# Two fused transformer layers: the work between layer zero and layer one dealt in another order

## What is computed

```
# layer 0: adaptive RMS norm, 8 query heads of 64, one key/value head, then a gated MLP of 2048
h   = x * rsqrt(mean(x*x) + 1e-6) * (ln1_w * (1 + cond @ ln1_tw.T))
q, k, v = h @ Wq.T, h @ Wk.T, h @ Wv.T        # q and k turned by their positions (rope)
x   = x + softmax(q k' / 8) v @ Wo.T
h2  = x * rsqrt(mean(x*x) + 1e-6) * (ln2_w * (1 + cond @ ln2_tw.T))
x   = x + (silu(h2 @ Wg.T) * (h2 @ Wu.T)) @ Wd.T
# layer 1: adaptive layer norm, 16 query heads of 32, 4 key/value heads through a latent of 128
y   = (x - mean(x)) * rsqrt(var(x) + 1e-5) * (1 + scale(cond)) + shift(cond)
q   = y @ Wq.T;  c = y @ Wkd.T;  k, v = c @ Wku.T, c @ Wvu.T
x   = x + softmax(q k' / sqrt(32)) v @ Wo.T
```

## Time and profile before

| what | value |
|---|---|
| median of 3 runs | 871.74 us (870.44, 871.74, 877.64) |
| the profiled execution | 878.93 us |
| span of its instructions | 877.1 us |
| TensorE busy in the span | 850.0 us (97%) |
| mean granted TensorE clock | 0.988 |

### The profile page before, as it was taken

One profiled execution on the slowest core, in us unless ns is written; L12 is line 12 of the kernel. 1 busy time (PEld: TensorE's weight loads), 2 busy tenths in 40 slices (PEclk: granted clock), 3 DMA queues, 4 the chain that ended last, 5 costly groups with the idle time before them and its releaser, 6 DMA issues.

```text
span 877.1 us, 15477 instructions
## 1 busy us (share of the span) xinstructions
PE 850.0 (97%) x5864; PEld 707.8 (81%) x5864; DVE 596.7 (68%) x877; ACT 443.1 (51%) x819; POOL 404.3 (46%) x320
## 2 busy tenths in 40 slices
PE   9798999999999999999999899999999999999997
PEld 6686888888888888888787788888878878887885
DVE  6686466766765766666457777876757857768874
ACT  4665445455445455444447456465463454445652
POOL 2456546455454455547357446354344434422330
PEclk9899999999999999999999999999999999999998
DMA  9901534534523524524534346446245264240001
GB/s 341 347 30 41 160 104 141 159 102 138 169 101 103 175 94 117 175 95 122 192 121 120 119 136 186 146 137 187 93 157 161 97 181 136 76 119 13 26 26 37
DMA packets 114297, 113.53 MB, mean 129 GB/s; under 512 B 57520, under 2 KB 80048, under 8 KB 114224
## 3 DMA queue, kind: packets, MB, share of 16 engines
q1 hardware_dynamic: 113504, 112.45, 40.2%
q10 hardware_dynamic: 720, 0.09, 0.1%
HBM read 88.15 MB, written 24.38 MB: 128 GB/s over the span
## 4 chain that ended last, share of the span: by engine, by line
PE 74%; DVE 8%; issue 6%; DMA 4%; ACT 3%; POOL 3%; SPq 1%; POOLq 0%; ACTq 0%; DVEq 0%
PE ps L684 23%; PE ps L686 22%; PE ps L685 22%; DMA turned_q<-tq 2%; PE ps L798 2%; PE ps L964 1%; DVE ex L1410 1%; DMA rwd<-WdT 1%; PE ps L730 1%; PE ps L721 1%; PE ps L775 1%; PE ps L941 1%; POOL qkr L592 1%; POOL qkr L591 1%; DMA pT<-turned_p 1%
## 5 line engine op out<-in xcount | busy, mean ns | idle before, releaser
L684 PE MATMUL ps<-h2h,guh 128*128 128x512 f32 x512 | 205.5, 401 | 3.1 <-issue 2.2
L686 PE MATMUL ps<-h2l,guh 128*128 128x512 f32 x512 | 201.1, 393 | 0.0
L685 PE MATMUL ps<-h2h,gul 128*128 128x512 f32 x512 | 201.0, 393 | 0.0
L544 POOL TENSOR_TENSOR gul<-rgu,guh 128x1024 fp32r<-128x1024 f32 x64 | 160.5, 2508 | 68.4 <-ACT guh L1746 68.4
L549 POOL TENSOR_TENSOR wdl<-rwd,wdh 128x512 fp32r<-128x512 f32 x64 | 82.9, 1296 | 145.3 <-ACT wdh L1754 145.3
L1309 DVE TENSOR_TENSOR xres<-ps,xres 128x512 f32<-128x512 f32 x128 | 87.6, 685 | 65.9 <-PE ps L686 65.4
L684 PEld LDWEIGHTS ps<-h2h,guh 128*128 128x128 f32 x512 | 96.9, 189 | 24.8 <-issue 3.9
L686 PEld LDWEIGHTS ps<-h2l,guh 128*128 128x128 f32 x512 | 96.9, 189 | 21.2
L685 PEld LDWEIGHTS ps<-h2h,gul 128*128 128x128 f32 x512 | 96.9, 189 | 19.7
L684 PE MATMUL ps<-wdh,ah 128*128 128x512 f32 x256 | 100.3, 392 | 2.8 <-DVE al L1304 1.7
L685 PE MATMUL ps<-wdh,al 128*128 128x512 f32 x256 | 99.7, 389 | 0.0
(11 more groups left out here) (178 smaller groups left out, 1676.9 us busy)
## 6 DMA issues: line engine op xcount, KB each, us to landing
rgu<-gu SPq DMA_DIRECT2D x64, 512.0 KB, 4.8
rwd<-WdT SPq DMA_DIRECT2D x64, 256.0 KB, 4.1
turned_q<-tq SPq DMA_DIRECT2D x20, 320.0 KB, 2.7
qkT<-turned_q SPq DMA_DIRECT2D x20, 320.0 KB, 3.7
turned_p<-tp SPq DMA_DIRECT2D x9, 512.0 KB, 2.6
pT<-turned_p SPq DMA_DIRECT2D x9, 512.0 KB, 3.9
xt<-xT SPq DMA_DIRECT2D x16, 256.0 KB, 3.5
out<-xres SPq DMA_DIRECT2D x15, 256.0 KB, 3.6
```

The source lines that it names most:

```text
L544: pool.tensor_tensor(gul[i][:, :], rgu[i][:, :], guh[i][:, :], ALU.subtract).then_inc(m_gul, 1)
L684: pe.matmul(dst, lh, rh, start=start, stop=False)
L685: pe.matmul(dst, ll, rh, start=False, stop=False)
L686: return pe.matmul(dst, lh, rl, start=False, stop=stop)
```

## The change

It touches the steps s = 15 to u = 0, SP's order in steps 0 to 8 and DVE's in step 9. No instruction is added or taken away on any engine, and the pieces keep their order; only what stands between them moves.

- `FILL1`: step -1 has (4, 2, 2, 2, 2) in place of (4, 4, 0, 4, 0), step 0 has (4, 2, 4, 2, 0) in place of (4, 2, 2, 2, 2). Both still have 12. Step 9 had five zeros and now falls to the default of five zeros.
- s = 15: ACT's `norm1(0)` stands behind the first fill, DVE's `turn_y(0)` behind the second, SP's `y_away(0)` behind the second, directly ahead of `y_back(0)`.
- u = 0 to 8: SP does `probs_back1(u)` ahead of `y_away(u+2)`. In u = -1 nothing changes by this.
- u = 9: DVE does its first two pieces (`add_down` parts 0 and 1 of the last pair) ahead of `rope_mul1(10)` and not behind it.

```diff
-FILL1 = {-1: (4, 4, 0, 4, 0), **{u: (4, 2, 2, 2, 2) for u in range(0, 9)}, 9: (0, 0, 0, 0, 0)}
+FILL1 = {-1: (4, 2, 2, 2, 2), 0: (4, 2, 4, 2, 0), **{u: (4, 2, 2, 2, 2) for u in range(1, 9)}}
 
@@ SP, steps s
                     queries_back(s + 1)
+                fill(pieces, f2)
                 if s == NT - 1:
                     y_away(0)
-                fill(pieces, f2)
-                if s == NT - 1:
                     y_back(0)
@@ SP, steps u
                 if 0 <= u < TAIL:
                     probs_away1(u)
+                    probs_back1(u)
                 if u < TAIL:
                     y_away(u + 2)
-                if 0 <= u < TAIL:
-                    probs_back1(u)
-                if u < TAIL:
                     y_back(u + 2)
@@ DVE, steps u
                     turn_probs1(u)
+                if u == TAIL:
+                    fill(pieces, 2)
                 if in_layer(u + 1):
                     rope_mul1(u + 1)
                 if u == TAIL:
-                    fill(pieces, 2)
                     probs_T1(u)
@@ ACT, steps s
-                if s == NT - 1:
-                    norm1(0)
                 fill(pieces, f1)
                 if s > HEAD and in_layer(s + 1):
                     values(s + 1)
+                if s == NT - 1:
+                    norm1(0)
```

## The result

The changed kernel takes 880.12 us (median of 13 runs, 875.45 to 882.11), the kernel before 872.79 us (median of 13, 868.95 to 879.70). The ratio is 1.0071 with a 95% interval of 1.0048 to 1.0093: slower by 4 to 8 us, where 3.2 us faster had been forecast. The profiled execution took 876.11 us (span 874.3), less than the 878.93 us of before. It is the spread of the runs that makes this so: the trace of before is one of its slowest executions, the trace of after one of the faster ones. A second trace of each was therefore taken; with them there are four to read.

A forecast was written before the change was run, and what follows sets the result against it. TensorE, busy in 97% of the span, was taken as the bound, leaving waits and low-clock stretches to remove. Terms -1.8 - 0.3 - 1.1 = -3.2 us, on the median 871.74, gave 868.5 us; range 863.5 to 874.5.

The forecast's parts named there:

- seam: From s = 15 to the gate behind the scores of step 1: 1.8 us faster, of 6.8 us removable.
- rounds: Steps u = 1 to 8: 0.3 us faster, from the second wait for probabilities; bounds -1.0 and +5.6 us.
- step 9: DVE's additions ahead of the rope: the 1.1 us wait of down 31,2 goes, 1.1 us faster.
- s = 15 and u = -1: Silu wait (0.9 us), queries' wait (1.7) and low clock of gate 37 (1.7) go; L1395 starts near 475.5.
- DVE in u = 0 and the scores of step 1: Scale 2.3 us earlier, still taking 3.42; scores of step 1 wait 3.8 us, to 505.5 in place of 508.21.
- second rival: In step 0 DVE's scale runs apart from POOL's subtraction, chain 2.2 us shorter: -5.4, 866.3 us; chance 0.10.
- third rival: Each round SP waits 2.6 us longer for y's store: rounds +5.6, net +2.4, 874.1 us; chance 0.16.
- The fourth: Seam keeps its time: scores of step 1 wait 5.5 us or clock falls twice; -0.3 to -1.4, 870.8; chance 0.17.
- The first: Both new waits fail to appear and all gains arrive: -10.6 us at most, some -9, 863 us; chance 0.09.

The follow-up runs named there:

- the three kernels with the queries first in the new fills: Whole change, queries' store ahead of y's fetch: 866.96 us; also y's store before probabilities' fetch: 867.48; or queries' store also before fill's weight load: 866.30.
- the norm alone: Kernel before with only the norm of tile 0 moved in s = 15 (ACT, DVE, SP): 870.58 us, ratio 0.9974.
- step 9 alone: Kernel before with only DVE's two pieces ahead of the rope in step 9: 872.42 us, ratio 0.9978.
- the kernel before with the queries first: Kernel before with SP's queries' store ahead of the fetch of y in steps -1 to 8: 877.16 us, ratio 1.0024.
- the two variants: Whole change, queries' store ahead of y's fetch, plus y's store before probabilities' fetch (867.48 us) or queries' store before the fill's weight load (866.30 us).

## Why the prediction was wrong

The sum was -1.8 (seam), -0.3 (rounds), -1.1 (step 9), and the gate behind the scores of step 1, with or without the low clock, was counted to the seam. In these terms the first trace of after has, against the first and the second of before: seam -4.5 and -0.7 up to the scores of step 1, with +1.7 behind them for the low clock; rounds +5.7 and +6.7 without that stretch; step 9 -1.3. One by one:

*Step 9: right.* -1.0 to -1.3 in the traces, -1.4 alone, by the mechanism named.

*s = 15 and u = -1: right in what it removed.* The silu wait, the queries' wait and the low clock of gate 37 all went. L1392 of step 0 was held back by `high_act(36)` behind the weight's cast, as said: `high_act(36)` starts 4.0 us behind the end of `high_y(1)` (I had counted 4.1), and L1392 2.6 us behind that (2.3). But the whole chain came 3.0 us sooner than I had put it (472.47 for 475.5); 1.7 of these the trace had ahead of s = 15, the rest I can't account for. One reading was incomplete: I called 2.5 and 1.7 us the two longest single waits of PE, and the full list also has two of 2.2 us, early in layer zero, which no edit touches.

*DVE in u = 0 and the scores of step 1: the mechanism right, the size not.* The chain was shorter than I counted (timeline of DVE, then of POOL, against the earlier trace rows):

```profile
481.66 1.22 DVE L1407 TENSOR_TENSOR ex<-ex,smx 128x1024 f32<-128x1024 f32 x1
482.91 2.02 DVE L1428 STREAM_TRANSPOSE tp<-ex 128x1024 f32<-128x1024 f32 x1
...
488.26 1.32 DVE L1421 STREAM_TRANSPOSE tq<-qkr 128x640 f32<-128x640 f32 x1 [0.26 <-POOL qkr L589]
```
```profile
482.05 3.10 POOL L541 TENSOR_TENSOR gul<-rgu,guh 128x1024 fp32r<-128x1024 f32 x1 [2.30 <-ACT guh L1743]
```

The scale took 1.22 us, the case of my second rival, though the reason that I gave there is not what happened: the two did start together, with the scale 0.4 us ahead. The queries' wait was 2.6 us and not 3.8. Against the trace of before the scores of step 1 came 6.2 us earlier (I had said 2.7), 4.5 of them in the seam. But that trace was not a typical one: against the second the seam gains 0.7 us up to these scores, and behind them 1.7 us go to the low clock. So against it the seam as a whole lost 1 us. The seam's own edits are not to blame: without the new order of SP the same seam takes 94.8 us, 2.4 less than in the second trace of before, and no low clock follows. Step 0's share of the new order took it back. I read a bound and a baseline off one execution, which I had noted to be 7 us over the median, and then put its difference on the median.

*Rounds u = 1 to 8: wrong, and this is the step that failed.* I had taken "equal within 0.6" for the landing of the queries' store, and 0.3 us of gain; the measured term is +5.7 to +6.7 us, or +7.4 to +8.5 with the low clock behind the scores of step 1. It was my third rival, at 0.16. The queries are stored 1.7 to 2.3 us later in each round (the rival said 2.3), well past the 0.7 us of slack that it named. Two sizes were off, both to the same side: y's store was to land 4.0 us after its own issue, with the fetch ahead of it at 3.8, and took 4.6 to 4.8, as that fetch itself became 0.4 longer; and from the issue of y's fetch to the landing of the queries' store I estimated 4.8 us from a step in which the queue was idle, and in step 1 it is 5.5 (528.67 to 534.13), over steps 1 to 7 5.6 on average. I priced a quiet queue from one quiet example and let it cancel against a full one. Together they make 1.3 to 1.6 us, which is small in one round, but it exceeds the slack and is paid in most of eight. The rule of the Trainium skill that I cited (DMA: Bandwidth & Descriptors, Queues, rings and completion order: a completion is reported only after every earlier write of that DMA engine) agrees with the traces: the store moved behind a 4 us fetch went from 2.2 to 4.6 us. I used it to place the store, and not to ask who stands behind SP meanwhile.

*How the 7 us are made up in the first trace of after:* the waits of PE behind the scores of step 1 and up to those of step 9 sum to 7.4 us (queries 1.9, `al` 3.3, probabilities 2.2) where before had 2.6; the low clock behind the scores adds 1.7; the rest, about 1 us, is in the gaps too short for the list and the first matmul behind each wait. The `al` waits look like the same cause again: the down weights are loaded behind the queries' fetch in SP's program, and the three kernels with the queries first in the new fills have no wait for `al` at all.

*Rivals.* The third is what happened. Its 5.6 us for the rounds are close to the 5.7 to 6.7 measured without the low clock. Its net was +2.7 and not +2.4, as I had kept the 0.3 us of gain beside it. The 880.1 in place of its 874.1 comes from the low clock (it had 877.5 with two such stretches) and from the seam, which I had credited with 1.8 us. The range ended at 874.5, short of its worse form. The fourth, a seam that keeps its time, was in part right: against the second trace of before the seam gains nothing once the low clock is counted. The first fell: the new wait at the scores of step 1 did appear.

## What to carry to other kernels

When two transfers are exchanged on a queue whose issuer waits for landings, look at what the issuer has behind each wait, not at the pair itself. Where the issuer must wait for a store before it can go on, keep long fetches from in front of that store; better, issue whatever is wanted next ahead of the wait, and the place of the store matters no longer. A lateness of a microsecond or two in a loop is to be compared with the slack of every round and multiplied. And take a second trace before a difference of a per cent is built on one, above all when its own time lies outside the runs.

## What the runs showed that I had not expected

**Who is first on two engines decides 2.2 us.** The scale of step 0 (`softmax_scale1`, DVE, 1024 columns) took 1.2 us in eleven of the fourteen traces and 3.42 us in three, and nothing between. In the trace of before POOL's subtraction starts at 486.03 and the scale at 486.32, 0.3 us later; in the second trace of the same kernel the scale is first, by 0.2 us, and POOL takes the longer (first fence: before, POOL; second: the second trace of before, DVE and POOL):

```profile
486.03 2.63 POOL L544 TENSOR_TENSOR gul<-rgu,guh 128x1024 fp32r<-128x1024 f32 x1 [0.18 <-ACT guh L1746]
```
```profile
484.23 1.21 DVE L1410 TENSOR_TENSOR ex<-ex,smx 128x1024 f32<-128x1024 f32 x1
...
484.43 3.28 POOL L544 TENSOR_TENSOR gul<-rgu,guh 128x1024 fp32r<-128x1024 f32 x1 [0.67 <-ACT guh L1746]
```

The 3.42 us came in three of the four traces in which the clock had fallen behind the queries' wait of step 0 (before, the norm alone, step 9 alone) and in none without that fall. The fourth, of the kernel before with the queries first, had the fall and 1.22 us: `silu` was late there, and the scale started 0.4 us ahead of POOL. That the fall brings the two engines into the other order is possible, but was not tried by itself. In steps 1 to 8 the scale took 2.9 to 3.4 us in all fourteen, and 1.2 from step 9 on, where the MLP's subtractions are over. An experiment that parts the two in steps 1 to 8 was not made.

**The low clock makes much of the spread.** Among the runs of before, those with a mean granted clock of 0.996 have a median of 870.5 us (34 runs), those with 0.990 one of 877.9 (16 runs). Among the changed kernel's, 0.994 goes with 876.0 (8 runs) and 0.990 with 880.7 (8 runs). At an equal clock the changed kernel stays slower: 876.0 against 872.5 at 0.994, 879.5 (7 runs) against 873.8 (28 runs) at 0.992, 880.7 against 877.9 at 0.990. So 3 to 6 of the 7 us are there whatever the clock, and the clock makes the rest at most.

Part of this spread has nothing to do with the change. From the scores of step 10 to the end, eleven of the fourteen traces take 72.9 or 73.0 us. The other three (the first of before, the second of after, and one of the two variants, with y's store first) take 75.6, and in these the granted clock is 0.50 for some 6 to 7 us within this stretch, as here in the first trace of before (busy time by stretch):

```profile
866.60:873.20 6.60, 5.92 (x45) 5.29 (x43) 1.22 (x3) 1.33 (x3) 0.00 (x0) 0.50 0.11 40
```

Which waits are followed by a fall is not settled. Ahead of scores, all four of 2.4 to 2.8 us were, and of the eight of 1.4 to 1.8 us four were; the three of 2.4 to 2.6 us ahead of a context were not.
